# Splitting the 176 contraction rows of a mixture-of-experts down product as 112 + 64 instead of 88 + 88

## The chip, the cores and the metric

The kernel runs on one core of one Trainium2 chip. The metric is the device time of one execution in microseconds, the median over the runs. A NeuronCore has five engines that run side by side and meet through semaphores: TensorE (PE in the profile; its weight loads are shown apart as PEld), VectorE (DVE), ScalarE (ACT), GpSimd (POOL) and SyncE (SP, which here only issues DMAs). TensorE contracts over the partition rows of its operands and writes PSUM. All large matrices are fp32.

## The reference

Four residual layers follow each other on x of 8 x 256 tokens by 256 features: cross attention, a mixture of experts, cross attention with extra keys, and a second expert layer. The change touches only the second of them, whose core is:

```python
def _L0_ffn_ref(hidden_states, gate_w, gate_bias, Wg, Wu, Wd, Sg, Su, Sd):
    H = 256; I = 176; E = 64; TOP_K = 8
    ...
    def _mlp(x, gw, uw, dw):
        return jax.nn.silu(x @ gw.T) * (x @ uw.T) @ dw.T
    x = hidden_states.reshape(B * S, H)
    rw = _route(x, gate_w, gate_bias)
    expert_out = jax.vmap(lambda gw_, uw_, dw_: _mlp(x, gw_, uw_, dw_))(Wg, Wu, Wd)
    routed = jnp.einsum('eth,te->th', expert_out, rw)
    shared = _mlp(x, Sg, Su, Sd)
    return (routed + shared).reshape(B, S, H)
```

Each token goes to 8 of 64 experts, so `_mlp` is computed only for the chosen pairs of token and expert (the routed part). Every token also goes through the shared expert, whose inner width is 2 x 176 = 352. The product with `dw` is "the down product": it contracts over 176 (routed) or 352 (shared) inner features.

## The kernel before

**Stages.** Attention for 16 tiles of 128 tokens (0 to about 97 us in the profile), the router together with the shared expert for the first 13 tiles ("early", NEARLY, to about 195 us), the routed experts (to about 618 us), the shared expert for the last 3 tiles ("late", NLATE), then the second attention and the second expert layer, which the change doesn't touch.

**Routed work.** The pairs of token and expert are sorted by expert into 320 halves of 64 rows; two halves make a block of 128 rows, 160 blocks (NRUN) in all. The first half (FIRST, rows 0 to 63) and the second (SECOND, rows 64 to 127) of a block may belong to two experts. So each product of a block is two calls of 64 columns of the array: FIRST with the weights where they were loaded (`wgu`, `wdn`, one of 8 slots, addressed through a register), SECOND with a copy of the other expert's weights (`wguB`, made by VectorE, and `wdnB`, made by ScalarE). In the profile such a pair is shown as `88*64` or `128*64` (rows and columns of the array in use), and every fp32 call has two matmul records. One call of each kind and its partner run side by side in the two column halves.

A block goes through these steps:

- GpSimd gathers its rows into `xg`; TensorE turns them (`c_transpose`, L1425), ScalarE copies them to `xT` (L1104).
- `c_up`: two contraction steps of 128 rows for gate and up together (352 columns), into PSUM bank 2 or 3.
- ScalarE: silu of the gate half into `sg` (`c_gate`, L1119). VectorE: the product with the up half into `hC` (`c_product`, L2268).
- `c_transpose_h`: two transposes of 88 columns each into bank 4 or 5 (L1430); VectorE copies them to `hT` (`c_copy_hT`, L2274), 88 partitions by 2 x 128.
- `c_down`: two contraction steps of 88 rows into bank 6 or 7; the last increments `c_dn`.
- ScalarE scales by the routing weight into `yC` (`c_y_out`, L1129) and issues the store to `y_rows` (`store_y`, L1108), which first waits until `yC` is written.

**Order.** Every engine has its own instruction stream, written by hand in groups of two blocks (`c_group(j)`, j even). On TensorE a group is: `c_down(j-3)`, `c_up(j)`, `c_up(j+1)`, `c_down(j-2)`, the transposes of the rows of blocks j+2 and j+3, then the transposes of h of blocks j and j+1. ScalarE and VectorE have matching groups. A wait blocks what stands behind it on the same engine; a DMA issue occupies the issuing engine's sequencer.

**Weights.** SP loads one expert after another into the 8 slots: `load_gu` when the old expert's up products are done, `load_dn` (L584) when its `c_dn` count is reached. `w_ld` counts 32 for a full slot.

**Shared expert.** For a tile: two up products (L1334 with `wgu,nTB`), four transposes of 88 columns, one copy of 88 x 512 to `hT` on ScalarE (L1062), and four contraction steps of 88 rows (`s_down`), with 256 output columns over all 128 array columns. The product with silu is on GpSimd (L746). During tiles 8 to 11 TensorE also multiplies the one-hot tables `ohP`, `ohB` that VectorE builds (L2228) and ScalarE numbers (L1067); from them the gather indices `idx` come. The late tiles do the same through semaphores of their own (`l_*`), with the product on VectorE.

## Time and profile before

| What | us |
|---|---|
| median of 3 runs | 1356.46 (1355.89 to 1359.14) |
| span of the profiled execution | 1352.5 |
| difference of the two, outside the span | 4.0 |
| TensorE busy | 1232.8 (91%) |
| VectorE busy | 913.6 (68%) |
| ScalarE busy | 754.3 (56%) |
| GpSimd busy | 502.9 (37%) |
| mean granted TensorE clock | 0.974 of 2.4 GHz |

The span is the time from the first to the last instruction of one profiled execution. A share of busy time is an average over stages with different limits, so the table doesn't tell what bounds a stage; for that one looks at windows of a stage, at who waits for whom there, and at the rows of one period in order of time. Durations of matmuls overlap, since they are pipelined: what a matmul costs is the distance from its start to the next one's start. Before a VectorE, ScalarE or GpSimd instruction, the bracket in a timeline row says how long the engine sat idle and who released it.

### The profile page before, as it was taken

The page shows a single profiled execution, that of the slowest core. Times are in us where ns is not written, and L with a number is a line of the kernel's source. Part 1 is how long each engine was busy: PE and PEld are TensorE (multiplying, and loading weights), DVE is VectorE, ACT ScalarE, POOL GpSimd, SP SyncE. Part 2 cuts the span into 40 slices and gives each one's busy share as a digit, 9 for nine tenths or more (in the row PEclk, how much of TensorE's full clock was granted, in tenths as well). Part 3 has the DMA queues.
Part 4 walks back from the last instruction along what each step waited for, and adds up shares of the span by engine and source line. Part 5 has one row for each costly group of instructions (what it writes and reads, how often), then busy time and mean ns, then how long its engine had stood idle before and what let it go on. Part 6 is the DMA issues. An engine that isn't in the chain of part 4 may idle for free. (4 is left out here: it accounts for less than half of the span.)

```text
span 1352.5 us, 32733 instructions
## 1 busy us (share of the span) xinstructions
PE 1232.8 (91%) x9060; PEld 928.9 (69%) x9062; DVE 913.6 (68%) x2392; ACT 754.3 (56%) x1930; POOL 502.9 (37%) x549
## 2 busy tenths in 40 slices
PE   4999999999999999997578888989878999999998
PEld 3887665555555555554456676767756899999997
DVE  7988857555555555554486876767785766676666
ACT  2444566556565555652447876778764544444443
POOL 1012354333343333424876677774711111011010
PEclk9999999999999999999779999999999999999999
DMA  5013216777576557534432222221200000000000
GB/s 117 0 57 105 78 40 193 228 210 231 174 222 188 172 162 230 179 96 131 131 88 64 67 66 57 63 59 39 96 24 10 16 17 16 16 16 16 8 0 17
DMA packets 99465, 125.02 MB, mean 92 GB/s; under 512 B 28595, under 2 KB 84371, under 8 KB 99347
## 3 DMA queue, kind: packets, MB, share of 16 engines
q1 hardware_dynamic: 62339, 59.05, 15.1%
q0 software_dynamic: 13968, 43.53, 11.6%
q10 hardware_dynamic: 23040, 20.98, 4.6%
q8 instruction: 59, 0.97, 0.3%
q14 instruction: 59, 0.48, 0.1%
HBM read 95.58 MB, written 27.95 MB: 91 GB/s over the span
## 5 line engine op out<-in xcount | busy, mean ns | idle before, releaser
L779 POOL DMA_INDIRECT xg<-n_rows,idx x160 | 163.3, 1021 | 242.3 <-DVE wS L2262 198.7
L1334 PE MATMUL ps<-wgu,xT 128*64 x640 | 202.9, 459 | 0.4 <-ACT xT L1104 0.3
L1334 PE MATMUL ps<-wdn,hT 88*64 (+1 forms) x768 | 199.1, 385 | 4.5 <-ACT hT L1168 2.4
L1334 PE MATMUL ps<-wguB,xT 128*64 128x352 f32 x640 | 202.9, 459 | 0.0
L1212 ACT ACTIVATE pD<-ps,nmx 128x333 f32<-128x333 f32 x256 | 139.2, 547 | 83.7 <-DVE nmx L2443 72.6
L2443 DVE TENSOR_REDUCE nmx<-ps 128x1 f32<-128x333 f32 x256 | 126.2, 496 | 87.1 <-PE ps L1334 86.1
L1334 PE MATMUL ps<-wdnB,hT 88*64 88x256 f32 x640 | 168.4, 386 | 0.0
L1702 PE MATMUL ps<-ident,pD 128*128 128x128 f32 x768 | 135.0, 287 | 35.6 <-DVE pT L2449 33.2
L1334 PEld LDWEIGHTS ps<-wdn,hT 88*64 88x64 f32 (+1 forms) x768 | 104.6, 145 | 74.5 <-issue 43.2
L813 POOL DMA_INDIRECT yg<-y_rows,slotG x128 | 123.3, 963 | 80.8 <-DMA y_rows<-yC 26.4
L1334 PEld LDWEIGHTS ps<-wgu,xT 128*64 128x64 f32 x640 | 87.3, 137 | 85.4 <-issue 73.2
L1702 PEld LDWEIGHTS ps<-ident,pD 128*128 128x128 f32 x768 | 98.7, 146 | 52.5 <-issue 21.0
L1129 ACT ACTIVATE yC<-ps,wS 128x256 f32<-128x256 f32 x160 | 76.0, 475 | 98.4 <-PE ps L1334 97.0
L1334 PE MATMUL ps<-kM,qP 128*128 128x334 f32 x256 | 109.1, 427 | 9.5 <-ACT pD L1212 9.1
L2274 DVE COPY hT<-ps 88x256 f32<-88x256 f32 x160 | 67.0, 419 | 71.9 <-PE ps L1334 67.8
L1300 ACT ACTIVATE sl<-ps 128x256 f32<-128x256 f32 x128 | 48.1, 383 | 104.8 <-PE ps L1334 101.5
L2610 DVE TENSOR_TENSOR gg<-sl,ps 128x256 f32<-128x256 f32 x128 | 52.9, 419 | 77.4 <-ACT sl L1300 76.6
L2262 DVE TENSOR_SCALAR wS<-xg 64x1 f32 x320 | 47.2, 147 | 83.3 <-ACT yC L1129 65.5
L1113 ACT COPY wdnB<-wdn 88x512 f32 x160 | 98.6, 617 | 0.0
L1119 ACT ACTIVATE sg<-ps 128x176 f32<-128x176 f32 x160 | 50.8, 318 | 72.6 <-PE ps L1334 70.5
L1334 PEld LDWEIGHTS ps<-wguB,xT 128*64 128x64 f32 x640 | 87.3, 137 | 0.0
L2255 DVE COPY wguB<-wgu 128x704 f32 x160 | 81.3, 550 | 2.2 <-POOLq L773 2.2
(323 smaller groups left out, 3300.7 us busy)
## 6 DMA issues: line engine op xcount, KB each, us to landing
wgu<-in_wgu SPq DMA_DIRECT2D x64, 352.0 KB
y_rows<-yC ACTq DMA_DIRECT2D x160, 128.0 KB
wdn<-in_wdn SPq DMA_DIRECT2D x64, 176.0 KB
xg<-n_rows,idx POOLq DMA_INDIRECT x160, 3.7
kraw<-in_kD SPq DMA_DIRECT2D x8, 308.0 KB, 2.8
x<-in_x SPq DMA_DIRECT2D x4, 512.0 KB, 5.0
n_rows<-nB SPq DMA_DIRECT2D x4, 512.0 KB, 4.1
yg<-y_rows,slotG POOLq DMA_INDIRECT x128, 4.7
```

Source lines behind the costliest of these rows:

```text
L779: pool.indirect_dma_start(out=xg[:, b % XS, :], out_offset=None, in_=n1_rows, in_offset=bass.IndirectOffsetOnAxis(ap=idx[:, b:b + 1], axis ...
L813: pool.indirect_dma_start(out=yg[:, q, k, :], out_offset=None, in_=y_rows, in_offset=bass.IndirectOffsetOnAxis(ap=slotG[:, u:u + 1], axis= ...
L1113: act.copy(wdnB[:, n % 2, :, :], wdn[:, bass.ds(slot, 1), :, :].rearrange("p s c n -> p (s c) n")).then_inc(c_dnB, 1)
L1119: act.activation(sg[:, n % 2, :], ps[:, 2 + n % 2, 0:I0], ACT.Silu).then_inc(c_silu, 1)
L1129: act.activation(yC[:, n % YS, :], ps[:, 6 + n % 2, 0:D], ACT.Copy, scale=wS[:, n % XS:n % XS + 1]).then_inc(c_y, 1)
L1212: act.activation(pD[:, k % AHEAD, :], ps[:, score_bank(k), 0:NK1], ACT.Exp, bias=nmx[:, k:k + 1], accum_out=den[:, k // TB // HG1, head_of ...
L1334: return pe.matmul(o, lhsT, rhs, start=start, stop=stop, **kw)
L1702: last = pe.transpose(ps[:, 5 + k % 2, c * P:(c + 1) * P], pD[:, k % AHEAD, at:at + P], ident[:])
L2255: dve.tensor_copy(wguB[:, n % 2, :, :], wgu[:, bass.ds(slot, 1), :, :].rearrange("p s c n -> p (s c) n")).then_inc(c_guB, 1)
L2274: dve.tensor_copy(hT[:, n % 2, :, :], ps[0:IC, 4 + n % 2, 0:2 * P].rearrange("p (c n) -> p c n", c=2)).then_inc(c_hT, 1)
L2443: dve.tensor_reduce(nmx[:, k:k + 1], ps[:, score_bank(k), 0:NK1], AX, ALU.max, negate=True).then_inc(d_mx, 1)
L2610: dve.tensor_tensor(gg[:, f % 2, int(second), :], sl[:, int(second), :], ps[:, f % 4, SEQ:2 * SEQ], ALU.mult).then_inc(f_g2 if second else ...
```

## The change

**Routed down product.** The 176 rows are split as 112 (KMAIN) and 64 (KREM). `c_main(m)` is one contraction step over 112 rows, FIRST and SECOND, for each block. The rests of 64 rows of two blocks lie in the two halves of the partitions: rows 0 to 63 for the even block, 64 to 127 for the odd one. `c_rest(m)` issues four calls for the pair, each on a 64 x 64 quarter of the array, into banks 6 and 7. For this the two blocks' h lie side by side in `hC` so that three transposes of 128 columns serve both; `c_copy_hT` copies 128 x 384 once for a pair; the odd block's product on VectorE is written in two pieces (112 and 64 columns). `wdn` holds 128 rows of the expert in chunk 0 and the last 64 rows twice in chunk 1, once for each half of the partitions, so `load_dn` is three DMAs and 256 rows instead of one and 176 rows. The first expert's rests are copied by VectorE into `wdnF` (two copies of 64 x 256 in a group, `second_rest`), because a slot is no longer held by a register on TensorE when they are used.

**Order.** TensorE's group becomes: `c_rest(j-4)`, `c_up(j)`, `c_up(j+1)`, `c_main(j-2)`, `c_main(j-1)`, transposes of rows, transposes of h for the pair. On ScalarE both outputs and stores of the pair j-4 now stand ahead of the first silu, and the copy to `wdnB` between the two.

**Shared down product.** The 352 rows go as 128 + 128 + 96: three transposes, a copy of 128 x 384, three contraction steps. The late tiles use the early tiles' semaphores.

The core of the diff, in the order of the file (`c_group` is ScalarE's, `second_rest` and what follows it VectorE's):

```diff
-IC = I0 // 2
+KREM = P // 2
+KMAIN = I0 - KREM
+REM_AT = KREM
+MAIN_AT = (0, KMAIN + 2 * KREM)
+SHC = 3
+SH_K = (P, P, 2 * I0 - 2 * P)
+LD_W = 64
...
             def load_dn(e, q):
-                sp.dma_start(wdn[:, NSH + q, :, :], A["wdn"][e].rearrange("(c p) n -> p c n", p=IC)).then_inc(w_ld[q], 16)
+                sp.dma_start(wdn[:, NSH + q, 0, :], A["wdn"][e][0:P, :]).then_inc(w_ld[q], 16)
+                for at in (0, REM_AT):
+                    sp.dma_start(wdn[at:at + KREM, NSH + q, 1, :], A["wdn"][e][KMAIN:I0, :]).then_inc(w_ld[q], 16)
...
             def s_copy_hT(t):
                 act.wait_ge(s_th, t + 1)
                 after(act, c_dn, t)
-                act.copy(hT[:], ps[0:IC, 4, :].rearrange("p (f c n) -> p f c n", f=2, c=2)).then_inc(s_hT, 1)
+                act.copy(hT[:, 0, :, :], ps[:, 4, 0:SHC * P].rearrange("p (c n) -> p c n", c=SHC)).then_inc(s_hT, 1)
...
             def c_group(j, i, n):
 
-                lent = [m for m in (j - 1, j) if inside(m)]
-                if lent:
-                    second = table(act, slot_row[:, HALVES - 1, :], lent[0], len(lent), NSH, NSH + WSLOT - 1)
-                if inside(j - 3):
-                    c_y_out(j - 3, i, n - 3)
-                if inside(j - 1):
-                    second_dn(second[0], j - 1, n - 1)
-                if inside(j - 3):
-                    store_y(j - 3, n - 3)
                 if inside(j):
-                    for a in range(GROUP):
-                        c_gate(j + a, n + a)
-                if inside(j - 2):
-                    c_y_out(j - 2, i, n - 2)
+                    second = table(act, slot_row[:, HALVES - 1, :], j, GROUP, NSH, NSH + WSLOT - 1)
+                for m, at in ((j - 4, n - 4), (j - 3, n - 3)):
+                    if inside(m):
+                        c_y_out(m, i, at)
+                        store_y(m, at)
+                if inside(j):
+                    c_gate(j, n)
+                    second_dn(second[0], j, n)
+                    c_gate(j + 1, n + 1)
                 for a in range(GROUP):
                     c_copy_xT(j + 2 + a, n + a)
                 if inside(j):
-                    second_dn(second[-1], j, n)
-                if inside(j - 2):
-                    store_y(j - 2, n - 2)
+                    second_dn(second[1], j + 1, n + 1)
...
             def s_down(t, r):
                 after(pe, s_y, t)
                 pe.wait_ge(s_hT, t + 1)
-                for f in range(2):
-                    for c in range(2):
-                        last = mm(ps[:, 6, 0:D], hT[:, f, c, :], wdn[:, f, c, :], f == 0 and c == 0, f == 1 and c == 1)
+                for c, rows in enumerate(SH_K):
+                    last = mm(ps[:, 6, 0:D], hT[0:rows, 0, c, :], wdS[0:rows, c, :], c == 0, c == SHC - 1)
                 last.then_inc(c_dn, 1)
...
-            def c_down(m):
+            def c_main(m):
 
                 slot = slots[m]
                 pe.wait_ge(c_dnB, m + 1)
-                pe.wait_ge(c_hT, m + 1)
+                pe.wait_ge(c_hT, m // GROUP + 1)
                 if m == 0:
                     pe.wait_ge(s_y, NEARLY)
                 after(pe, c_y, m - 1)
-                for c in range(2):
-                    mm(ps[FIRST, 6 + m % 2, 0:D], hT[:, m % 2, c, FIRST], wdn[:, bass.ds(slot, 1), c, :], c == 0, c == 1, skip_group_check=True)
-                    last = mm(ps[SECOND, 6 + m % 2, 0:D], hT[:, m % 2, c, SECOND], wdnB[:, m % 2, c, :], c == 0, c == 1, skip_group_check=True)
-                last.then_inc(c_dn, 1)
+                turned_h = hT[0:KMAIN, m // GROUP % 2, m % GROUP, :]
+                mm(ps[FIRST, 6 + m % 2, 0:D], turned_h[:, FIRST], wdn[0:KMAIN, bass.ds(slot, 1), 0, :], True, False, skip_group_check=True)
+                mm(ps[SECOND, 6 + m % 2, 0:D], turned_h[:, SECOND], wdnB[0:KMAIN, m % (2 * GROUP), 0, :], True, False, skip_group_check=True)
+
+            def c_rest(m):
+
+                pe.wait_ge(c_dnF, m + GROUP)
+                for a in range(GROUP):
+                    rows = slice(a * REM_AT, a * REM_AT + KREM)
+                    turned_h = hT[rows, m // GROUP % 2, GROUP, :]
+                    mm(ps[FIRST, 6 + a, 0:D], turned_h[:, FIRST], wdnF[rows, m // GROUP % 2, :], False, True, skip_group_check=True)
+                    mm(ps[SECOND, 6 + a, 0:D], turned_h[:, SECOND], wdnB[rows, (m + a) % (2 * GROUP), 1, :], False, True, skip_group_check=True).then_inc(c_dn, 1)
...
+            def second_rest(slot, a, n):
+
+                rows = slice(a * REM_AT, a * REM_AT + KREM)
+                dve.tensor_copy(wdnF[rows, n // GROUP % 2, :], wdn[rows, bass.ds(slot, 1), 1, :].rearrange("p s n -> p (s n)")).then_inc(c_dnF, 1)
...
+                if n % GROUP == 0:
+                    last = dve.tensor_tensor(hC[:, 0:I0], sg[:, n % 2, :], ps[:, 2 + n % 2, I0:GU], ALU.mult)
+                else:
+                    dve.tensor_tensor(hC[:, MAIN_AT[1]:MAIN_AT[1] + KMAIN], sg[:, n % 2, 0:KMAIN], ps[:, 2 + n % 2, I0:I0 + KMAIN], ALU.mult)
+                    last = dve.tensor_tensor(hC[:, I0:I0 + KREM], sg[:, n % 2, KMAIN:I0], ps[:, 2 + n % 2, I0 + KMAIN:GU], ALU.mult)
+                last.then_inc(c_h, 1)
```

**Where it moves instructions.** Line numbers after the change are 6 to 12 higher. TensorE, from the transposes at the end of a group to the next group's first up product, before (one transposed h is 88 wide, one down product is two rows `wdn` and two rows `wdnB`):

```order
L1425 MATMUL ps<-ident,xg 128x128 x4
L1430 MATMUL ps<-ident,hC 88x128 x4
L1334 ISA
L1334 MATMUL ps<-wdn,hT 64x256
L1334 MATMUL ps<-wdnB,hT 64x256
L1334 ISA
L1334 MATMUL ps<-wdn,hT 64x256
L1334 MATMUL ps<-wdnB,hT 64x256
L1334 ISA
L1334 MATMUL ps<-wgu,xT 64x352
L1334 MATMUL ps<-wguB,xT 64x352
```

TensorE at the same place, after:

```order
L1431 MATMUL ps<-ident,xg 128x128 x4
L1582 MATMUL ps<-ident,hC 128x128 x2
L1583 MATMUL ps<-ident,hC 128x128
L1340 MATMUL ps<-wdnF,hT 64x256
L1340 MATMUL ps<-wdnB,hT 64x256
L1340 MATMUL ps<-wdnF,hT 64x256
L1340 MATMUL ps<-wdnB,hT 64x256
L1340 ISA
L1340 MATMUL ps<-wgu,xT 64x352
L1340 MATMUL ps<-wguB,xT 64x352
```

One whole down product stood between the transposes and the up products; the rests of two blocks stand there now, with three transposes of h ahead of them, not four.

ScalarE, from the first output of a group to the second, before, with the semaphores that each row waits for:

```order
L1126 REGISTER_ALU [waits c_dn]
L1129 ACTIVATE yC<-ps,wS 128x256 [waits c_st1,c_w]
L1113 ISA [waits w_block]
L1113 COPY wdnB<-wdn 88x512
L1108 ISA [waits c_y]
L1108 DMA y_rows<-yC 128x256
L1117 REGISTER_ALU
L1119 ACTIVATE sg<-ps 128x176 [waits c_h,c_gu]
L1117 REGISTER_ALU
L1119 ACTIVATE sg<-ps 128x176 [waits c_h,c_gu]
L1126 REGISTER_ALU [waits c_dn]
L1129 ACTIVATE yC<-ps,wS 128x256 [waits c_st2,c_w]
```

ScalarE after, from the store of the group's first output to the second silu:

```order
L1120 ISA [waits c_y]
L1120 DMA y_rows<-yC 128x256
L1138 REGISTER_ALU [waits c_dn]
L1141 ACTIVATE yC<-ps,wS 128x256 [waits c_st3,c_w]
L1120 ISA [waits c_y]
L1120 DMA y_rows<-yC 128x256
L1129 REGISTER_ALU
L1131 ACTIVATE sg<-ps 128x176 [waits c_h,c_gu]
L1125 ISA [waits w_block]
L1125 COPY wdnB<-wdn 128x512
L1129 REGISTER_ALU
L1131 ACTIVATE sg<-ps 128x176 [waits c_h,c_gu]
```

The second output and its store have moved from behind the two silus to ahead of them, and a copy to `wdnB` from behind the first output to between the silus.

## Rows read from the trace of the kernel before

**Rows 1.** 40 us of the routed stage: busy PE, PEld, DVE, ACT, POOL; clock; DMA share; GB/s.
```profile
280.00:320.00 40.00, 40.00 (x306) 23.14 (x302) 23.44 (x78) 24.05 (x62) 15.31 (x15) 1.00 0.75 220
```

**Rows 2.** TensorE in order of time, one group's end and the next one's start.
```profile
302.11 0.46 PE L1334 MATMUL ps<-wgu,xT 128*64 x1
...
302.41 0.38 PE L1334 MATMUL ps<-wdn,hT 88*64 x1
...
303.06 0.38 PE L1334 MATMUL ps<-wdn,hT 88*64 x1
...
303.37 0.66 PE L1425 MATMUL ps<-ident,xg 128*128 128x128 f32 x4
303.87 0.60 PE L1430 MATMUL ps<-ident,hC 128*88 128x128 f32 x4
304.40 0.43 PE L1334 MATMUL ps<-wdn,hT 88*64 x1
304.40 0.43 PE L1334 MATMUL ps<-wdnB,hT 88*64 88x256 f32 x1
304.66 0.38 PE L1334 MATMUL ps<-wdn,hT 88*64 x1
...
305.31 0.46 PE L1334 MATMUL ps<-wgu,xT 128*64 x1
```

**Rows 3.** The tile `wdnB`: first and last of the routed down products.
```profile
L1334 PE MATMUL ps<-wdnB,hT x640: 377/379/430, 202.2 to 618.0; 88*64 88x256 f32 x160
```

**Rows 4.** ScalarE and its DMA issues in order of time, same place; issue durations min/median/max.
```profile
300.50 0.47 ACT L1129 ACTIVATE yC<-ps,wS 128x256 f32<-128x256 f32 x1 [0.60 <-PE ps L1334]
300.87 0.60 ACT L1113 COPY wdnB<-wdn 88x512 f32 x1
301.14 0.55 ACTq L1108 DMA_DIRECT2D y_rows<-yC  x1
...
301.86 0.32 ACT L1119 ACTIVATE sg<-ps 128x176 f32<-128x176 f32 x1 [0.38 <-PE ps L1334]
...
302.62 0.32 ACT L1119 ACTIVATE sg<-ps 128x176 f32<-128x176 f32 x1 [0.45 <-PE ps L1334]
...
303.63 0.47 ACT L1129 ACTIVATE yC<-ps,wS 128x256 f32<-128x256 f32 x1 [0.69 <-PE ps L1334]
...
L1108 ACTq DMA_DIRECT2D y_rows<-yC x160: 338/338/551, 204.0 to 618.9; - x160
```

**Rows 5.** VectorE in order of time, same place; then groups by line, 240 to 600 us.
```profile
302.97 0.34 DVE L2268 TENSOR_TENSOR hC<-sg,ps 128x176 f32<-128x176 f32 x1 [0.16 <-ACT sg L1119]
303.26 0.97 DVE L2255 COPY wguB<-wgu 128x704 f32 x2
304.29 0.42 DVE L2274 COPY hT<-ps 88x256 f32<-88x256 f32 x1
...
L2262 DVE TENSOR_SCALAR wS<-xg 64x1 f32 x272 | 40.3, 148 | 75.7 <-ACT yC L1129 62.7 <-issue 5.8
```

**Rows 6.** TensorE released by VectorE's product, at the routed stage's end.
```profile
614.10 0.34 DVE L2268 TENSOR_TENSOR hC<-sg,ps 128x176 f32<-128x176 f32 x1 [0.85 <-ACT sg L1119]
...
614.50 0.64 PE L1430 MATMUL ps<-ident,hC 128*88 128x128 f32 x4
...
615.07 0.43 PE L1334 MATMUL ps<-wdn,hT 88*64 x1
```

**Rows 7.** TensorE and ScalarE in the shared stage, in order of time.
```profile
159.08 0.71 PE L1334 MATMUL ps<-ohB,ohP 128*128 128x160 f16 x8 [1.69 <-ACT ohP L1067]
...
167.05 1.97 PE L1334 MATMUL ps<-wdn,hT 88*128 88x256 f32 x8 [0.58 <-ACT hT L1062]
...
157.80 4.25 ACT L1067 ACTIVATE ohP<-ohP,id 128x1024 f16<-128x1024 f16 x4
```

**Rows 8.** What follows the routed stage, in order of time.
```profile
618.95 0.34 ACTq L1108 DMA_DIRECT2D y_rows<-yC  x1
...
650.34 1.09 PE L1663 MATMUL ps<-ident,nS 128*128 128x128 f32 x4 [14.92 <-DVE nS L2430]
```

More of the change, by code:

```diff
@@ L1443, in s_transpose_h @@
                 after(pe, s_hT, t)
[L1444 to L1446 removed]
+                transpose_h(4).then_inc(s_th, 1)
             def s_step(t, r, i):
```

120 lines of the change are left out of this document (62 added, 58 removed).

## The prediction

> **What bounds the kernel now.** I read the windows of the routed stage first, because most of the change lies there. In 40 us TensorE is busy for 40.00 us at the full clock, VectorE and ScalarE for about 23 and 24, the DMA engines at 0.75 [rows 1]. A busy TensorE is not yet one at its limit, so next I read one group (two blocks) in order of time and measured from start to start [rows 2]. Two calls that share the array's column halves start together (304.40 and 304.40), and the next record of a down product follows 0.215 us later (302.41 to 303.06 is three steps, 0.65). An up product's record lasts 0.295 (302.11 to 302.41; I use 0.2935, the mean of a longer run of such steps). A transpose takes 0.109: four in 0.60, of which the last one's own 0.27 is counted once. Where the kind of tile changes there is a loss: from the last down record at 303.06 to the first transpose at 303.37 it is 0.31, not 0.215, and the transposes need 0.05 more at their start; from the last transpose (303.87 + 3 x 0.109 = 304.20) to the down product 0.20, not 0.109, and that one's first step is 0.26, not 0.215. That is 0.15 a change of kind. The sum of a group: 8 x 0.2935 + 8 x 0.215 + 8 x 0.109 + 2 x 0.15 = 2.35 + 1.72 + 0.87 + 0.30 = 5.24 us. The trace has 5.27 (the last down record before an up product at 305.31 - 0.215 and the same one group earlier; and 202.2 to 618.0 in [rows 3] is 79 groups of 5.26). So TensorE is the limit of this stage, with nothing idle in it.
>
> **TensorE's part of the change.** The two whole down products (8 steps of 0.215) become two main products of 112 rows (4 steps) and the rests of both blocks. If the rests' four calls run side by side in four quarters of the array, they take 2 steps. That is minus 2 x 0.215 = 0.43. Three transposes and not four: minus 0.11. One change of kind more (transposes, rests, ups instead of transposes, down, ups): plus 0.15. TensorE would need 5.27 - 0.39 = 4.88 us for a group. No row shows row halves at work together, so the rests' price is bounded by 2 steps and 4 steps (0.43 and 0.86); I take 2, since the column halves do exactly this (two calls start at 304.40), and since the halves of the rows write different banks, 6 and 7.
>
> A rule bears on this. The change of kind costs 0.15 in the rows [rows 2]. The Trainium skill, page "TensorEngine Tiling (Array Packing)", section "Key Properties", says that changing the tiling mode drains TensorE. Read to the letter, the rests could begin only when the last transpose's 0.27 us are over, 0.07 later than the 0.20 measured; the rows show a softer loss. By the letter the sum below would be 79 x 0.07 = 5.5 us longer. The same page, "Gotcha 1: PSUM Pressure", wants different banks for different row tiles, which this change has.
>
> **ScalarE's part, the decisive one.** TensorE's saving counts only if its partners keep pace, and ScalarE's order has changed. Before, two silus came right after the up products; one output stood ahead of them and one behind. Now a group on ScalarE reads: output, store, output, store, silu, copy to `wdnB`, silu. The store is issued by ScalarE's own sequencer after the output is written, and the next output can't start before it. This makes a closed loop: the rests of pair j-4 start, both outputs, both stores, silu of j, copy, silu of j+1, product of j+1, transposes of the pair, and then the rests of the next pair. Its length, step by step:
>
> - rests' start to their end: 0.26 + 0.38 = 0.64 (first step and last record, [rows 2])
> - end of a down product (303.06 + 0.38) to the output (303.63): 0.19; output 0.47; its end (300.97) to the DMA issue (301.14): 0.17; issue 0.34 (median; only the row shown has 0.55); its end (301.69) to the next ScalarE instruction (301.86): 0.17 [rows 4]. First output and store: 0.19 + 0.47 + 0.17 + 0.34 + 0.17 = 1.34. Second: 0.47 + 0.17 + 0.34 + 0.17 = 1.15
> - silu 0.32, then the copy 0.60, then silu 0.32; neighbours overlap by 0.10 (output 300.50 + 0.47, copy at 300.87): 0.32 + 0.60 + 0.32 - 0.20 = 1.04
> - silu's end (302.94) to the product (302.97): 0.03. The product in two pieces: 176 columns are 0.34 [rows 5], a piece with 1 column 0.148 [rows 5], so about 0.0011 us a column: 112 are 0.27, 64 are 0.22, less 0.08 of overlap (an estimate, from ScalarE's 0.10 above): 0.41
> - product's end (614.44) to the first transpose (614.50): 0.06; to the down product (615.07) 0.57 with four transposes, so 0.46 with three [rows 6]
>
> Sum: 0.64 + 1.34 + 1.15 + 1.04 + 0.03 + 0.41 + 0.06 + 0.46 = **5.13 us**. This is longer than TensorE's own 4.88, so the loop sets the period, and TensorE will stand idle for about 0.25 us ahead of the transposes of h. Against 5.27 a group saves 0.14, times 79 groups: **-11 us**. The bounds: each of some twelve links is read to 0.01, and the overlaps may differ; I take 5.03 to 5.23, which is -19 to -3.
>
> **VectorE** gains work: the product's second piece (+0.15), two `wdnF` copies (64 x 256; nearer to the 0.148 of a tiny piece than to the 0.49 of 704 columns, half of 0.97, [rows 5]; about 0.25 each, less overlap, +0.4), a third table of registers (+0.3 to 0.5, in the sequencer, beside running copies); one copy of 384 columns replaces two of 256 (0.42 each; 0.55 against 0.84, -0.29), and with it goes the wait between the two. Net +0.6 on 3.1 busy of 5.27. It is hidden in its idle time, which was 2 us a group; the product isn't behind these copies, since they follow it. If that cover were gone, each 0.1 us would cost 8 us.
>
> **Weights.** `load_dn` moves 256 rows, not 176, in three issues: 64 experts x 80 KB = 5 MB more on a DMA share of 0.75 [rows 1], over 410 us about +0.04. The slot of an even block is given back one half group later (2 us) than before. TensorE never waited for weights in the rows; I cost it at nothing, and if the cover fails each late expert would stop both engines for a us or two.
>
> **The end of the routed stage.** The last pair needs main, an output before the second main (banks 6 and 7 must be free), rests, two outputs and two stores in a row, where before the last store came 4.5 us after the last product (614.44 to 618.95, [rows 6, 8]). By the same links: rests of 156 at +0.5, its outputs done at +1.8 and +3.0, main of 159 after that, rests of 158 at +3.6, outputs and stores until +5.8. **+1.3 us**, all on the path, because the gathers of `y_rows` follow.
>
> **The shared expert.** Each early tile loses one contraction step of two records (-0.43), one transpose (-0.11), and its `hT` copy shrinks. Up to tile 8 this is 0.54 x 8 = 4.3 us on TensorE. There TensorE had waited 1.69 for the first numbered table, and ScalarE began numbering only after the output of tile 7 [rows 7], which is TensorE's work. So most of it counts, until VectorE's fourth table is the limit: ScalarE's fourth numbering would end at about 158.7, not 162.05 (157.80 + 4.25): **-3.5**. The next three rounds (a tile and four tables each) lose 0.43 + 0.13 (the wait for `hT` was 0.58, [rows 7], and the copy is 0.13 shorter): **-1.7**. One more step in the last tile: **-0.5**. The late tiles gain nothing: TensorE waits 14.92 us for the norm after them [rows 8], which hangs on the gathers.
>
> **Sum.** -11 + 1.3 - 3.5 - 1.7 - 0.5 = -15.5 us. The profiled span of 1352.5 goes to 1337; outside it lie 4.0 us, which stay. Against the median: 1356.5 - 15.5 = **1341 us**.
>
> **The rivals.**
>
> *TensorE sets the period* (the loop is shorter than I summed, because the sequencer runs ahead where I put links in a row). Then a group takes 4.88: 79 x 0.39 = -31, with the rest -4.4: **1321**. For it: in the rows before, ScalarE had 2 us idle in a group. Against: each link of the loop is a true dependence or a measured issue.
>
> *The row halves don't run together.* The rests take 4 steps. Then TensorE needs 4.88 + 0.43 = 5.31, and the loop isn't longer (the even block's rest is done first): the routed stage stays as it was or gains 3 us too much, **1355** (+3 on -4.4). Against it: the column halves. The skill's page "TensorE: Matmul & The Clock Gate", Part 3, holds that matmuls start and end in program order; an order so strict that a call's second record holds back the next call would give this case, but in this trace calls whose partner has a second record still to come start together [rows 2].
>
> *ScalarE's loop is longer than before* and the kernel slower. The price is in the DMA issues: if alone between two outputs they take the 0.55 of [rows 4] instead of 0.34, the loop is 5.55, 0.28 over the old period: +22 - 4.4 = **1374**. It decides from a loop of 5.33 (where it eats the shared part's gain). A slow drain before the rests would add to it. Against: 0.34 is minimum and median of 160 issues, also for the one with nothing beside it (618.95, [rows 8]).
>
> *The change doesn't do what it says* in the shared stage (the tables, not TensorE, set that stage): only the 5 us there would go, 1346. It lies inside the range.
>
> **How the numbers follow.** My forecast (5.03 to 5.23, 1332 to 1350) has 0.52; TensorE's limit 0.20; no overlap of the rows 0.12; ScalarE slower 0.16. The likeliest gives 1341. The range reaches down to the TensorE case (1320) and up through the case without overlap (1356); what is left out is most of the slower case and a little below, 0.18. A measurement of this kernel can tell 0.3%, 4.1 us, from no change, so faster is below 1352.4: 0.52 + 0.20 + 0.04 = 0.76; same: 0.08 + 0.03 = 0.11; slower 0.13.
>
> **What would show it.** Right: in a group of the changed kernel TensorE has a gap of 0.2 to 0.3 us ahead of the h transposes, released by VectorE's product; the period is 5.1; the first silu starts 3.1 us after the rests, long after its up product. The four rests have two start times, 0.26 apart. Wrong: no such gap and a period of 4.9 (TensorE), four start times (no overlap), a DMA issue of over 0.5 in most groups (slower), waits of TensorE for `wguB` or of ScalarE for weights (my zero costs). For the shared part: the first routed down product some 5 us before the 202.2 of [rows 3].

## The result, and the profile after

The changed kernel takes **1347.99 us** (median of 4 runs, 1346.22 to 1348.78); the kernel before took 1357.53 in the same comparison (4 runs, 1355.89 to 1359.14). The ratio is 0.9925 with a 95% interval of 0.9905 to 0.9944. The forecast was 1341, with a range of 1320 to 1356: the sign and the range hold, the gain is 9.5 us where 15.5 were forecast.

Two rows say how far the routed stage is TensorE's own. The first is the same 40 us as [rows 1], the second the waits of TensorE's weight load for the product (engine, line, tile, what released it: us in total, times, longest), 240 to 600 us:

```profile
280.00:320.00 40.00, 39.12 (x304) 19.66 (x300) 25.35 (x95) 24.55 (x63) 16.17 (x16) 1.00 0.83 239
PEld ps L1582 <- DVE hC L2288: 20.1, 57, 1.3
```

TensorE was busy for 40.00 of 40 us and is now for 39.12: it waits 57 times, a third of a microsecond each, for VectorE's product. DMA has gone from 0.75 to 0.83.

TensorE in order of time, where the transposes of h end and the rests come (start, duration, engine and line, operation, tiles); it answers to [rows 2]:

```profile
302.57 0.66 PE L1431 MATMUL ps<-ident,xg 128*128 128x128 f32 x4
303.29 0.44 PE L1582 MATMUL ps<-ident,hC 128*128 128x128 f32 x2
303.56 0.27 PE L1583 MATMUL ps<-ident,hC 128*128 128x128 f32 x1
303.77 0.43 PE L1340 MATMUL ps<-wdnF,hT 64*64 64x256 f32 x1
303.77 0.43 PE L1340 MATMUL ps<-wdnB,hT 64*64 64x256 f32 x1
303.78 0.43 PE L1340 MATMUL ps<-wdnF,hT 64*64 64x256 f32 x1
303.79 0.43 PE L1340 MATMUL ps<-wdnB,hT 64*64 64x256 f32 x1
304.03 0.38 PE L1340 MATMUL ps<-wdnF,hT 64*64 64x256 f32 x1
```

All four quarters start within 0.02 us (303.77 to 303.79) and their second records 0.26 later: the row halves run together, as the column halves did. The transposes of x start at 302.57, and four steps of 0.109 later, at 303.01, those of h could start; they do at 303.29. That is the gap of 0.28.

ScalarE in the same group, and then in one of the groups at the stage's start. It answers to [rows 4]:

```profile
304.63 0.47 ACT L1141 ACTIVATE yC<-ps,wS 128x256 f32<-128x256 f32 x1 [0.42 <-PE ps L1340]
305.27 0.34 ACTq L1120 DMA_DIRECT2D y_rows<-yC  x1
305.79 0.47 ACT L1141 ACTIVATE yC<-ps,wS 128x256 f32<-128x256 f32 x1 [0.69 <-ACT yC L1141]
306.43 0.34 ACTq L1120 DMA_DIRECT2D y_rows<-yC  x1
306.94 0.32 ACT L1131 ACTIVATE sg<-ps 128x176 f32<-128x176 f32 x1 [0.67 <-ACT yC L1141]
...
307.66 0.32 ACT L1131 ACTIVATE sg<-ps 128x176 f32<-128x176 f32 x1
```

```profile
206.74 0.47 ACT L1141 ACTIVATE yC<-ps,wS 128x256 f32<-128x256 f32 x1
207.25 0.34 ACTq L1120 DMA_DIRECT2D y_rows<-yC  x1
207.69 0.47 ACT L1141 ACTIVATE yC<-ps,wS 128x256 f32<-128x256 f32 x1 [0.47 <-ACT yC L1141]
208.19 0.35 ACTq L1120 DMA_DIRECT2D y_rows<-yC  x1
208.65 0.32 ACT L1131 ACTIVATE sg<-ps 128x176 f32<-128x176 f32 x1 [0.48 <-ACT yC L1141]
```

This is the row pair to learn from. The work is the same, but from one output to the next it is 1.16 us at 304.63 and 0.95 at 206.74, and from the second output to the silu 1.15 and 0.96. From an output's end to its DMA issue it is 0.17 (305.10 to 305.27) and 0.04 (207.21 to 207.25). The first group lies in the rolled loop, where addresses and counts are computed in registers, the second in the part that is written out with constants. ScalarE's sequencer (q) has these rows on the lines of the store and of the output (count, durations in ns, first and last start):

```profile
L1120 ACTq FUSED_REGOPS  x128: 46/46/60, 231.9 to 562.3; - x128
L1138 ACTq ALU_OP  x112: 40/43/43, 236.5 to 561.7; - x112
```

The first is the register work of the two stores in the 64 groups of the loop, and none of it lies before or behind the loop; a `MOVE` of 0.03 us follows each. In the group above, `FUSED_REGOPS` and `MOVE` run between the first output's end and its store's issue (305.14 to 305.24), and an `ALU_OP` between the issue's end and the second output (305.65).

The period, from one group's first up product to the next one's, is 4.89 us in 14 groups (7 ahead of the loop, 7 behind it) and 5.15 to 5.45 in the 64 between; their mean is 5.23, with one of 6.14 where a single store's issue took 1.31 us. The very first period is 5.97. Before, it was 5.27 in all but the first two (6.15 and 5.32).

Where the time went, by marks in the two traces. The first rows are the up products, the stores, the first norm copies of the next stage and the last stage's outputs of the changed kernel (count, durations in ns, first and last start):

```profile
L1340 PE MATMUL ps<-wguB,xT x640: 459/459/510, 190.9 to 601.9; 128*64 128x352 f32 x160
L1120 ACTq DMA_DIRECT2D y_rows<-yC x160: 338/338/1310, 202.4 to 609.0; - x160
L1197 ACT COPY nTD<-ps x8: 576/582/593, 641.5 to 941.6; 128x512 f32<-128x512 f32 x8
L2665 DVE SCALAR_TENSOR_TENSOR yE<-ps,wE,x x16: 473/480/485, 1082.2 to 1344.0; 128x256 f32<-128x256 f32 x16
```

and the same of before (its stores stand in [rows 4] and [rows 8], last at 618.95):

```profile
L1334 PE MATMUL ps<-wguB,xT x640: 457/459/510, 193.7 to 613.2; 128*64 128x352 f32 x160
L1191 ACT COPY nTD<-ps x8: 576/582/593, 651.5 to 951.2; 128x512 f32<-128x512 f32 x8
L2640 DVE SCALAR_TENSOR_TENSOR yE<-ps,wE,x x16: 473/479/485, 1090.1 to 1349.5; 128x256 f32<-128x256 f32 x16
```

The changed kernel is ahead by 2.8 us at the first routed up product (193.7 to 190.9), by 10.0 at the last store (618.95 to 608.97), still by 10.0 and 9.6 at the first and last batch of the attention stage, by 7.9 at the last stage's first output (1090.1 to 1082.2), and by 5.5 at the end of the span (1352.5 to 1347.0). So 4.5 us of the gain are lost between these two executions in stages that the diff does not touch. The medians differ by 9.5 and the profiled executions by 5.5: 1.8 us lie outside a span, so the span of before, 1352.5, is 3.2 short of what its median gives, and the changed kernel's, 1347.0, is the longest of its four (1344.5 to 1347.0).

### The profile page after: what moved, and what is told of

The parts are those of the page before. It is cut to its first block and busy times, and to the rows that moved or that the text cites. A ratio compares the mean times of both kernels' runs of the same rounds, so it can differ in the third digit from the quotient of the medians.

```text
span 1347.0 us, 33002 instructions
## 1 busy us (share of the span) xinstructions
PE 1217.1 (90%) x8934; PEld 891.1 (66%) x8934; DVE 934.0 (69%) x2552; ACT 754.6 (56%) x1930; POOL 504.5 (37%) x550
## 5 line engine op out<-in xcount | busy, mean ns | idle before, releaser
L1340 PE MATMUL ps<-wgu,xT 128*64 x640 | 206.7, 465 | 0.1
L1340 PE MATMUL ps<-wguB,xT 128*64 128x352 f32 x640 | 206.7, 465 | 0.0
L1340 PEld LDWEIGHTS ps<-wgu,xT 128*64 128x64 f32 x640 | 81.0, 136 | 103.6 <-issue 102.6
L1340 PE MATMUL ps<-wdnB,hT 112*64 112x256 f32 (+1 forms) x640 | 135.0, 390 | 0.0
L1340 PE MATMUL ps<-wdn,hT 112*64 (+2 forms) x416 | 106.4, 380 | 4.4 <-ACT hT L1174 2.1
L1125 ACT COPY wdnB<-wdn 128x512 f32 x160 | 99.4, 621 | 0.0
L1340 PEld LDWEIGHTS ps<-wdn,hT 112*64 112x64 f32 (+2 forms) x416 | 61.1, 149 | 47.6 <-issue 29.2
L1340 PEld LDWEIGHTS ps<-wguB,xT 128*64 128x64 f32 x640 | 81.0, 136 | 0.0
L1340 PE MATMUL ps<-lT_h,b_h 128*128 128x256 f32 x256 | 73.8, 288 | 3.0 <-DVE gg L2635 3.0
```

Of the source, the lines that this page charges most:

```text
L1125: act.copy(wdnB[:, n % (2 * GROUP), :, :], wdn[:, bass.ds(slot, 1), :, :].rearrange("p s c n -> p (s c) n")).then_inc(c_dnB, 1)
L1340: return pe.matmul(o, lhsT, rhs, start=start, stop=stop, **kw)
```

## The experiments

The theory is the prediction's: a closed loop through ScalarE sets the period in the routed stage; in the shared stage the tables and the copy `hT` do. The changes below are all made to the changed kernel, unless said otherwise. Each run's ratio is to the kernel before in the same comparison (medians of 1355.66 to 1357.63), so ratios are what to compare; the changed kernel's is 0.9925.

**Does ScalarE's loop set the period?** Two edits shorten it in different places: e3 takes the copy to `wdnB` from between the silus, e4 puts both outputs ahead of both stores.

```diff
                 if inside(j):
                     c_gate(j, n)
-                    second_dn(second[0], j, n)
                     c_gate(j + 1, n + 1)
+                    second_dn(second[0], j, n)
```

```diff
                 for m, at in ((j - 4, n - 4), (j - 3, n - 3)):
                     if inside(m):
                         c_y_out(m, i, at)
+                for m, at in ((j - 4, n - 4), (j - 3, n - 3)):
+                    if inside(m):
                         store_y(m, at)
```

> The changed kernel, with ScalarE's copy to wdnB moved from between the two silus of a group to behind them. Theory A (ScalarE's loop of outputs, stores, silu, copy, silu sets the period of 5.2 us in the rolled groups): the loop is 0.5 shorter, 4.7, and TensorE's own 4.89 sets the period: 64 groups x 0.31 = 20 us less, 1328; the wait of TensorE for hC goes away. Rival B (VectorE's longer work or the weights' DMAs hold the group up): the period stays above 5.1, and the time at 1344 to 1348.

> The changed kernel, with both outputs of a group ahead of both stores on ScalarE, so that only one wait for a written output stands in the row. Theory A (ScalarE's loop): the two waits and the first issue no longer stand between the outputs, the loop is 0.3 shorter, 4.9, about TensorE's own 4.89: 15 to 20 us less, 1328 to 1333. Rival B (VectorE or weights): 1344 to 1348. If each store costs the same wherever it stands (0.34 of issue plus 0.17 after it), the loop is only 0.1 shorter: 1340.

Measured: e3 **1330.49** (ratio 0.9817, 0.9783 to 0.9852), e4 **1327.98** (0.9779, 0.9754 to 0.9804). The period is 4.89 in nearly all groups. In e3 it is 5.09 to 5.15 in every eighth, where the loop turns, and each of the two kernels has one late group, on which more below. The waits of `L1582` for the product, 20.1 us after the change, are 1.4 us in e3 from 310 to 580 us and none in e4. The theory holds; both edits end at the same bound, TensorE.

**Why is the loop long enough?** The rows above suggest the register work between outputs. In e9 nothing of ScalarE's order changes: its 64 groups are only written out with constants, on ScalarE alone.

```diff
-            with eng.Fori(1, NBLK // BLOCKS - 1) as i:
-                one_pass(BLOCKS * i, i, BLOCKS)
+            if eng is nc.scalar:
+                for i in range(1, NBLK // BLOCKS - 1):
+                    one_pass(BLOCKS * i, i, BLOCKS)
+            else:
+                with eng.Fori(1, NBLK // BLOCKS - 1) as i:
+                    one_pass(BLOCKS * i, i, BLOCKS)
```

> The changed kernel with one thing different: ScalarE's part of the routed stage is written out with constants for all its groups, where it was a loop with registers for 64 of the 79 groups and written out only for the first and the last. Nothing of its order changes. In the changed kernel the period is 4.89 us in the written-out groups and about 5.2 in the loop. Theory A: ScalarE's register work in the loop (the addresses of the stores and the counts to wait for, between two outputs) is what makes its own round longer than TensorE's work there. Then the period falls to 4.9 in the middle groups too, as if the outputs were first: 64 x 0.3 = 19 us less, about 1330, with a sure gain above 12 us. Theory B: what differs in the middle is VectorE's or TensorE's loop, or the traffic of the weights (which is less at the stage's ends). Then the period stays at 5.15 to 5.25 and the time at 1348. Between the two: each 0.1 us of the period is 6.4 us.

Measured: **1324.67** (0.9785, 0.9768 to 0.9802). The period is 4.89 in all but three of the middle groups. The second output now comes 0.97 after the first, as at the stage's start:

```profile
305.30 0.47 ACT L1145 ACTIVATE yC<-ps,wS 128x256 f32<-128x256 f32 x1 [0.60 <-PE ps L1344]
305.80 0.34 ACTq L1124 DMA_DIRECT2D y_rows<-yC  x1
306.27 0.47 ACT L1145 ACTIVATE yC<-ps,wS 128x256 f32<-128x256 f32 x1 [0.49 <-ACT yC L1145]
306.77 0.33 ACTq L1124 DMA_DIRECT2D y_rows<-yC  x1
307.20 0.32 ACT L1135 ACTIVATE sg<-ps 128x176 f32<-128x176 f32 x1 [0.46 <-issue]
```

Theory A is shown: what ScalarE's rolled code does in registers, 0.2 us for each of two stores, lifts its loop over TensorE's 4.89; VectorE and TensorE are still rolled in e9, and the period fell all the same. How the 0.2 divides between the arithmetic, the waits for counts held in registers and the store's address in a register is not shown, since e9 takes away all of them together. The Trainium skill, page "Advanced Engine Details and Errata", section "Sequencer Loop", says that the sequencer executes a control instruction itself, and that other engine instructions can be read and queued meanwhile. The rows agree as far as they go: from the silu to the copy behind it it is 0.21 us in the loop (306.94 to 307.15) and with constants (208.65 to 208.86), though the loop has a register instruction more there, while between an output and a store that hangs on it the register work is paid in full.

The gain is larger than the period gives. The changed kernel's first and last batch of attention lie 300.1 us apart (641.5 to 941.6), here 294.3:

```profile
L1201 ACT COPY nTD<-ps x8: 576/582/599, 621.4 to 915.7; 128x512 f32<-128x512 f32 x8
```

There the trace of the changed kernel has two stretches at half clock more (3.4 us each, at 809 and 898), and ScalarE stands longer where its loop turns, which it does twice: 2.75 at 805.97 after the change, 1.85 at 785.63 here.

```profile
805.97 0.54 ACT L1218 ACTIVATE pD<-ps,nmx 128x333 f32<-128x333 f32 x1 [2.75 <-issue]
```

```profile
785.63 0.54 ACT L1222 ACTIVATE pD<-ps,nmx 128x333 f32<-128x333 f32 x1 [1.85 <-issue]
```

This goes with the written-out code in every kernel here: e9 and e12 stand 1.8 to 2.0 us at both turns, have neither stretch and take 294.3 and 293.4; the twelve others, the kernel before among them, stand 2.5 to 2.9, have both stretches and take 299.2 to 301.5. That the shorter stand keeps the clock up fits the rows, but no run separates it; why the turn is shorter when another stage's code is written out stays open.

**What is the next bound?** In each of the faster kernels one group is late. VectorE and GpSimd in e9, in order of time (GpSimd's queue counts the experts whose weights have landed, `w_block`, ahead of a gather; SyncE's count at line 618 releases it):

```profile
300.19 0.53 DVE L2270 COPY wguB<-wgu 128x704 f32 x1 [3.49 <-POOLq L789]
300.78 0.95 POOL L795 DMA_INDIRECT xg<-n_rows,idx  x1 [4.43 <-SPq L618]
300.86 0.51 PE L1344 MATMUL ps<-wgu,xT 128*64 x1 [1.86 <-DVE wguB L2270]
```

An expert's weights are late once, and the group takes 7.60 us for 4.89. e3, e4 and the kernels e11 and e12 below have it at the same group (copy waits of 2.88, 3.96, 3.10 and 3.28), and e8 a milder one (6.08) one group earlier. At a period of 5.23 the weights kept pace; at 4.89, with a DMA share of 0.83, the cover that the prediction costed at nothing fails once. In e4 TensorE also ran at half clock for 3.4 us behind it.

**The shared part alone.** e5 is the kernel before with the three-pass shared product and nothing of the routed part. The core of its edit:

```diff
-                for f in range(2):
-                    for c in range(2):
-                        last = mm(ps[:, 6, 0:D], hT[:, f, c, :], wdn[:, f, c, :], f == 0 and c == 0, f == 1 and c == 1)
+                for c, rows in enumerate(SH_K):
+                    last = mm(ps[:, 6, 0:D], hT[0:rows, c, :], wdS[0:rows, c, :], c == 0, c == SHC - 1)
...
```

> The kernel before with the shared expert's part of the change alone: three transposes, a copy of 128 x 384, three contraction steps; the routed part as before. Theory A (what the changed kernel's trace shows: the first routed up product 2.8 us earlier, the late tiles hidden): 2.5 to 3 us less than before, 1354, period of a routed group 5.27. Rival (my forecast for this part): 5.5 to 6 us less, 1351.

Measured: 1352.32 (0.9972, 0.9958 to 0.9987). The first routed up product is at 190.0 against 193.7, the last store at 614.8 against 618.95: 3.7 to 4.1 us, between the two values expected and short of the 5.7 that were forecast for this part. In the routed stage the period is 5.27 again.

**The copy `hT`.** The prediction gave 1.7 us to three rounds of tables. e6 moves the copy ahead of the tables, so that nothing stands ahead of the down product.

```diff
+                    if f == 0 and not first:
+                        s_copy_hT(t - 1)
                     for n in tiles[2 * f:2 * f + 1]:
                         numbered(n)
-                    if f == 0 and not first:
-                        s_copy_hT(t - 1)
```

> The changed kernel with ScalarE's copy to hT ahead of the numbering of two one-hot tables in tiles 9 to 11 (it stood behind the first). Theory A (the three rounds with tables kept their 7.6 us because TensorE still waited 0.60 for that copy): the wait goes, and each round is 0.4 to 0.6 shorter, 1.5 us in all, 1346.5. Rival (ScalarE's numbering itself is the limit of a round): the wait only moves to the tables ohP, the rounds stay at 7.6 us and the time at 1348.

Measured: 1346.93 (0.9925, 0.99 to 0.9951), the changed kernel's ratio; the time can't tell the two expectations apart, the trace can. TensorE in one round, after the change and in e6:

```profile
172.78 1.53 PE L1340 MATMUL ps<-wdn,hT 128*128 128x256 f32 x6 [0.60 <-ACT hT L1074]
174.16 1.84 PE L1340 MATMUL ps<-ohB,ohP 128*128 128x160 f16 x24
176.32 0.71 PE L1340 MATMUL ps<-ohB,ohP 128*128 128x160 f16 x8 [0.32 <-ACT ohP L1079]
...
180.37 1.53 PE L1340 MATMUL ps<-wdn,hT 128*128 128x256 f32 x6 [0.60 <-ACT hT L1074]
```

```profile
170.81 1.46 PE L1340 MATMUL ps<-wdn,hT 128*128 128x256 f32 x6
172.11 1.27 PE L1340 MATMUL ps<-ohB,ohP 128*128 128x160 f16 x16
174.07 0.71 PE L1340 MATMUL ps<-ohB,ohP 128*128 128x160 f16 x8 [0.69 <-ACT ohP L1079]
175.10 0.71 PE L1340 MATMUL ps<-ohB,ohP 128*128 128x160 f16 x8 [0.32 <-ACT ohP L1079]
...
178.39 1.46 PE L1340 MATMUL ps<-wdn,hT 128*128 128x256 f32 x6
```

A round is 7.59 us in one (172.78 to 180.37) and 7.58 in the other. The wait for `hT` (0.60) is gone and one for a numbered table (0.69) stands in its place: the rival is right in that the wait only moves. But ScalarE isn't always busy either: of a round it works 5.84 us without a pause and then waits 1.75 for the next up product,

```profile
178.29 0.32 ACT L1086 ACTIVATE sg<-ps 128x176 f32<-128x176 f32 x1 [1.75 <-PE ps L1340]
```

which TensorE starts behind the table that ScalarE numbered last (176.32). So the round is a closed loop of silu, ScalarE's numbering, the last table's product and the up product, and TensorE's shorter down product only makes TensorE wait more (0.60 + 0.32, before 0.58). VectorE, which builds the tables, is busy for 6.33 of 7.60 us.

**The half clock.** After the change TensorE runs at 1.2 instead of 2.4 GHz from 157.4 to 164.2 (6.8 us; before 160.3 to 163.7), after waits of 1.69, 0.33 and 1.00 us for tables. e7 fills them with seven unused products of the identity.

```diff
                 for n in range(TABLE_TILES * (t - TABLE_AT), TABLE_TILES * (t - TABLE_AT + 1)):
+                    if t == TABLE_AT:
+                        keep_busy(0, (4, 1, 2, 0)[n])
                     onehots(n, n % OHS)
```

> The changed kernel with seven unused products of the identity on TensorE in the gaps ahead of the first three tables at 153 to 158 us. Theory A (these gaps, which the change made earlier but not shorter, are followed by 6.8 us at half the granted clock, and that costs about 2 us of the shared part's gain): the clock stays at 1.0 from 150 to 190 us, the first routed up product comes 2 us earlier (189), 1346. Rival (the half clock there is chance, or costs nothing because the tables are waited for): no difference, 1348.

Measured: 1344.45 (0.9923, 0.9898 to 0.9949), a ratio that can't be told from the changed kernel's; the trace can, with the first routed up product at 188.4 and not 190.9; 1.7 of these 2.5 us lie in this stage. The clock column (0.91, then 1.00) of 150 to 190 us, after the change and in e7:

```profile
150.00:190.00 40.00, 33.58 (x214) 24.54 (x212) 28.79 (x44) 25.80 (x47) 13.70 (x17) 0.91 0.04 9
```

```profile
150.00:190.00 40.00, 35.26 (x239) 25.70 (x238) 28.09 (x43) 26.49 (x48) 17.03 (x20) 1.00 0.04 10
```

All four kernels with these products keep the full clock here. But e9 keeps it without them, through the same waits:

```profile
155.10 0.71 PE L1344 MATMUL ps<-ohB,ohP 128*128 128x160 f16 x8 [1.69 <-ACT ohP L1083]
156.14 0.71 PE L1344 MATMUL ps<-ohB,ohP 128*128 128x160 f16 x8 [0.32 <-ACT ohP L1083]
157.85 0.71 PE L1344 MATMUL ps<-ohB,ohP 128*128 128x160 f16 x8 [0.99 <-ACT ohP L1083]
...
150.00:190.00 40.00, 32.39 (x225) 23.24 (x223) 28.55 (x43) 26.48 (x48) 17.34 (x19) 1.00 0.04 10
```

and e3 kept it too. Of the eight kernels with the new shared part and without the added products, four run 6.8 us at half clock here, two 3.4 (e5, e10) and two none. From the first table's product to the next down product it is 9.8 to 9.9, 8.9 and 8.1 us in them, so the waits are a risk of up to 1.7 us, not a certain cost.

**Together.** e8 has the edits of e3, e4, e6 and e7.

> The changed kernel with four edits: both outputs ahead of both stores, the copy to wdnB behind both silus, the copy to hT ahead of the tables, and the seven unused products. Theory A: TensorE's 4.89 us sets every routed group, as with either of the first two edits alone (they don't add up), and the shared part's two edits add 2 to 3.5 us: 1324 to 1326. Rival (the two edits of the routed part add up, because ScalarE's loop still sets the period with one of them): the period goes under 4.85 and the time to 1320 or less.

Measured: 1326.77 (0.9767, 0.9739 to 0.9795), not to be told from e4 alone (0.9779). The two edits of ScalarE's order don't add up, since either one is enough for TensorE to be the bound. The shared part's two edits show in the traces only: from that stage's first up product to the first routed one it is 76.4 us in e8 and 78.0 in e4, but e8's stage began 3.4 us later.

**The last stage, which nobody touched.** The second region of SBUF grew from 106496 to 106528 bytes, and the tensors behind it moved by 32. e1 pads the changed kernel by 32 bytes more, e2 the kernel before by 32.

```diff
-        sb("region2", [P, max(size_b, size_d, size_f) // 4])
+        sb("region2", [P, max(size_b, size_d, size_f) // 4 + 8])
```

> The changed kernel with 32 bytes of padding per partition ahead of the second SBUF region, which the change had moved by 32 bytes. Theory A (placement): in the last stage, which the change doesn't touch, TensorE's steps go back from 0.117 to 0.1135 us and a batch from 38.5 to 38.2 us, so 2 to 3 us less than the changed kernel, 1345 to 1346. Rival (the last stage varies from chip to chip or run to run): 0.117 stays or both kernels of this call show the same step, and the time stays at 1348.

> The kernel before with the same 32 bytes of padding, nothing else. Theory A (placement): last stage's step 0.117, a batch 38.5 us, 2 to 3 us more than before, 1359 to 1360. Rival (varies by run): no difference from before, 1356 to 1358.

Measured: e1 1350.43 (0.9954, 0.9937 to 0.9971), e2 1358.52 (1.0012, 0.9994 to 1.003). The pad makes the last stage slower in both, so an alignment to 64 bytes is refuted, and the place matters. e10 then undoes the move in the changed kernel by laying a one-column tensor into a free column of another.

```diff
-            padv = s("padv", [P, 1])
...
-            eB = s("eB", [P, HGROUPS])
+            eB = s("eB", [P, HGROUPS + 1])
```

> The changed kernel with one thing different: a tensor of one column (padv) lies in an unused column of another (eB), which makes the second region 32 bytes smaller, 106496 as before the change, so that the tensors behind it lie where they did before the change. Theory A (the place of the tensors in SBUF sets the step of TensorE in the last stage: 0.1150 us before the change, 0.1171 moved by 32 bytes, 0.1193 moved by 64): the step is 0.1148 to 0.1152 again, a batch of the last stage takes 38.2 us and not 38.5, and the time falls by 2.5 us, to about 1345.5. Theory B (the step was changed by something else that the change brought, and the two kernels with an extra pad fell in with it by chance): the step stays at 0.117 and the time at 1348.

Measured: 1345.25 (0.9934, 0.9917 to 0.995). The last stage's outputs, first and last start, for e10 (0 bytes moved), e2 (32) and e1 (64); the changed kernel's and before's rows stand above:

```profile
L2664 DVE SCALAR_TENSOR_TENSOR yE<-ps,wE,x x16: 473/480/484, 1080.8 to 1340.3; 128x256 f32<-128x256 f32 x16
```

```profile
L2640 DVE SCALAR_TENSOR_TENSOR yE<-ps,wE,x x16: 473/479/484, 1091.9 to 1353.7; 128x256 f32<-128x256 f32 x16
```

```profile
L2665 DVE SCALAR_TENSOR_TENSOR yE<-ps,wE,x x16: 473/479/484, 1080.1 to 1344.6; 128x256 f32<-128x256 f32 x16
```

Moved by 0: 259.4 us before and 259.5 in e10. By 32: 261.8 after and 261.8 in e2. By 64: 264.5 in e1. The other kernels fall in: 261.7 to 261.8 in e3, e4, e6, e7, e8 and e9, moved by 32, and 259.5 in e11 and e12, moved by 0. The time as a whole can't tell 2.4 us here, since e10's ratio and that of the changed kernel overlap; the stage can.

**The best versions.** e11 is e4 with the unused products and the place of e10; e12 is e9 with those two.

> Three edits of the changed kernel together: both outputs ahead of both stores, seven unused products of the identity ahead of the first three tables of the shared stage, and the tensors behind the second region placed as before the change. If the three are independent, as they lie in three stages: 1348 less 20 (outputs first), 3.5 (kept busy) and 2.5 (place) is 1322. If the middle one is again worth nothing beside the first, as the run with all four edits suggests (1326.8 against 1328.0 with the outputs alone), 1324.5 to 1325.5.

> The changed kernel with ScalarE's part of the routed stage written out, seven unused products of the identity ahead of the first three tables of the shared stage, and the tensors behind the second region placed as before the change. The version with the first edit alone took 1324.7; in it the attention stage after the routed one took 294.3 us from its first to its seventh batch against 300.1 in the changed kernel, with two stretches at half clock fewer and ScalarE standing 2.0 and not 2.8 us where its loop turns. Theory A (that gain comes with the written-out code, whatever else is changed): attention 294 to 295 again; less 2.5 for the place and 0 to 3 for the kept-busy products: 1319 to 1322. Theory B (it was a hair's breadth case of the clock, by chance on the good side): attention 300 to 301 again, about 1326 with the outputs-first version's time of 1326.4 as the nearest neighbour.

Measured: e11 1326.39 (0.9798, 0.978 to 0.9816), higher than both of its expectations; e4 had 1327.98, so most of the two small gains isn't seen in the time (the ratios, 0.9798 and 0.9779, overlap). e12 **1320.43** (6 runs, 0.9726, 0.9702 to 0.9751), and its attention stage takes 293.4 us (nTD at 621.4 to 914.8): that gain comes with the written-out code again, theory A, and the time lies in the range that theory A gave. It is the fastest, 37 us under the kernel before.

## Why the prediction was right, and where it was off

**TensorE's part: right.** 4.88 us were forecast for a group, 4.89 are measured where nothing else binds. The rests take 2 steps. The Trainium skill, page "TensorE: Matmul & The Clock Gate", Part 3, "The mechanism", shows calls on different tiles starting some 4 ns apart although they keep program order, and the four starts here (303.77, 303.77, 303.78, 303.79) agree with that; the rival built on program order was a wrong reading of it. The change of kind of tile costs what the rows gave: the last transpose of h starts at 303.56 and lasts 0.27, the rests start at 303.77, 0.06 ahead of its end. A drain by the letter would have had them at 303.83.

**ScalarE's loop: right for the loop, wrong for the rest.** Link by link, forecast and measured (304.63 to 310 and the rows above): first output and store 1.15 and 1.16; second 1.15 and 1.15; silus and copy 1.04 and 1.04 (306.94 to 307.66, + 0.32); the down product's end to the output 0.19 and 0.20; h transposes to rests 0.46 and 0.48 (303.29 to 303.77). The sum is 5.18, not 5.13, and the mean over 64 groups 5.23. The gap of 0.25 ahead of the transposes of h is 0.28, and the first silu starts 3.2 us after the rests, where 3.1 was named. The rival of a slower loop hung on issues of 0.55 us; all but the one of 1.31 stayed near 0.34. But all rows of the sum came from the rolled loop, register work included, and were used for all 79 groups. In 14 of them the two distances are 0.2 shorter each, so that the loop is about 4.8 (an estimate: 5.18 less 0.4) and TensorE's 4.89 binds. The term was -11; from the first group's up products to the last one's it is -8.6 (417.5 to 408.9): 64 x 0.047 = 3.0, 14 x 0.38 = 5.3, and 0.2 in the first two groups. That -8.6 comes so near to -11 is partly luck. By the forecast the 64 groups of the loop should have given 9.0 and the 14 others 2.0; the 14 that another bound sets gave most of the gain. The step that failed is reading "the DMA issue" as 0.17 + 0.34 + 0.17 and calling it ScalarE's issue: 0.2 of these 0.68 were register work, and could be taken away (e9).

**The routed end: right.** +1.3 forecast; from the last up product to the last store it is 7.0 us and was 5.7.

**The shared part: -5.7 forecast, -2.8 measured.** Up to the first table it is as forecast: from the stage's first up product (112.26 before, 112.84 after) to that table it was 46.8 us and is 42.5, 4.3 less, though the table itself comes only 3.7 earlier (159.08 in [rows 7], 155.34), since the stage began 0.6 later in this execution. In e9, where the clock stays up, it is also as forecast behind the fourth (the next down product at 163.24 against 167.05: -3.8). After the change it stands at 165.20: the longer half clock eats 1.7 of it (9.86 us from the table to that product, 8.14 in e9). The prediction did not ask what the clock does when TensorE has less to do between the same tables. The three rounds gave 0.1 each and not 0.56: the step took the wait for `hT` as the one that ends last, and behind it stood the round's own loop (e6). The sign that was named, the first routed down product some 5 us before 202.2, failed with it: it starts at 199.3, 2.9 before. These are single executions; in the other traces with the new shared part the first routed up product starts at 188.4 to 192.8.

**VectorE, weights: right at this period.** Costed at nothing, and nothing is seen (the wait for weights appears only in the faster kernels). VectorE's added work was overstated: the terms of the engine itself, without the registers' table, come to +0.26 a group, and its busy time grew by 20.4 us over 80 groups (913.6 to 934.0), about 0.26 each, where the prediction wrote +0.6.

**"What lies outside the span stays": off.** 4.0 us were taken from a median that is not the profiled execution's time. In the runs whose span is known the time is 1.7 to 1.9 above it (1347.0 and 1348.78 for the changed kernel's profile). The forecast of 1341 doesn't hang on it, since it is the median less 15.5 either way, but the sum's reference, one execution, and the median it was set against are 2.2 us apart for no reason in the kernel.

**Not forecast at all:** 1.7 us more between attention's last batch and the last stage (138.9 before, 140.6 after), where the clock is at half for longer (one stretch of 10.2 us for 6.8, one more of 3.4), and 2.4 us in the last stage from the place of its tensors. Most of the 1.7 belongs to this execution and not to the change: e1, e6, e7 and e10, with the same instructions there, take 139.2 to 139.4. With the loop's 2.4 and the shared part's 2.9 these make up the difference of the two profiles to the forecast (-15.5 and -5.5) to within 0.6.

## What to carry to other kernels

Where an engine's own issue stands on the critical loop, compare the same instructions in a rolled and in a written-out stretch before pricing them: here 0.4 us of 5.2 was register work, and writing out one engine's loop was worth more than the change itself (from the routed stage's first group to its last it took 417.5 us before, 408.9 after the change and 390.7 in e9). When a bound moves by a few per cent, sum the partner's whole round, but take each link from the stretch where it is to be used. And a saving in work between two fixed events, such as tables that another engine makes, turns into waiting, and may cost the clock.

## What the runs showed of the hardware

- Four calls on the 64 x 64 quarters of the array start within 0.02 us of each other and take two steps of 0.26 and 0.38 together, as two column halves do.
- On ScalarE in a rolled loop the sequencer puts 0.17 us between an output and the issue of its store, 0.04 with constants, and 0.18 and 0.10 between the issue and the next output; the issue itself is 0.34 in both.
- ScalarE stood 2.5 to 2.9 us at each of two loop turns of the attention stage in twelve kernels, and 1.8 to 2.0 in the two whose ScalarE code for the routed stage is written out. Why is open.
- The last stage, nearly all TensorE, takes 259.4, 261.8 and 264.5 us with the same instructions when the tensors behind the second region lie 0, 32 and 64 bytes further, in 13 kernels. Why is open; only these three places were tried.
- The granted clock fell to half at 157 us, in the shared stage, after waits of 1.69, 0.33 and 1.00 us in some kernels and stayed full after much the same waits in others (e9 has 1.69, 0.32 and 0.99; e3 kept it too).
